# Sixteen ring places for gathered edge tiles, a fourth product bank and selector numbers from SBUF, in a four-layer graph network

## What is computed

```python
# layer 0: two relational convolutions (8 relations, 4 bases)
m   = sum(comp[etypes][:, b, None] * (h @ basis[b])[src] for b in range(4)) * norm[:, None]
h   = segment_sum(m, dst, num_segments=n) + bias + h @ loop_w
# layer 1: one relational convolution, 32 relations, 8 bases (same form, no loop)
# layer 2: mean of the neighbours and two dense products
# layer 3: four blocks of attention over the edges, each followed by a dense block
```

## Time and profile before

| | us |
|---|---|
| median of 3 runs | 3173.16 (3171.28 to 3173.49) |
| the profiled execution | 3168.56 |
| its span | 3167.1 |
| L0a, first step to last | 47.7 to 328 |
| L0b, first gather to the next load of weights | 522.0 to 798.4 |
| L1, first gather to the end of the turning | 927.9 to 1223 |
| PE busy in the span | 2981.4 (94%) |
| mean granted clock of PE | 0.985 of full speed |

### The profile page before, as it was taken

One profiled execution on the slowest core, in us unless ns is written; L12 is line 12 of the kernel. 1 busy time (PEld: TensorE's weight loads), 2 busy tenths in 40 slices (PEclk: granted clock), 3 DMA queues, 4 the chain that ended last, 5 costly groups with the idle time before them and its releaser, 6 DMA issues.

```text
span 3167.1 us, 44248 instructions
## 1 busy us (share of the span) xinstructions
PE 2981.4 (94%) x14658; PEld 2175.7 (69%) x14658; DVE 2092.7 (66%) x5078; ACT 1276.3 (40%) x2250; POOL 1166.5 (37%) x938
## 2 busy tenths in 40 slices
PE   5898998999979999999999999999999999999999
PEld 3333675444753356876458998789988899789987
DVE  7999323887348864255367678667776777767777
ACT  4666432001340033342154455345543555435554
POOL 4666236665356643441104022511135101441022
PEclk8999998999989999999999999999999999999999
DMA  2555523565236643324003001210014001130012
GB/s 81 161 163 162 174 78 122 164 170 156 79 115 169 175 129 102 96 76 145 21 30 107 12 34 50 84 53 15 31 50 129 15 8 64 43 103 15 8 64 79
DMA packets 129587, 279.39 MB, mean 88 GB/s; under 512 B 22727, under 2 KB 45575, under 8 KB 128339
## 3 DMA queue, kind: packets, MB, share of 16 engines
q0 software_dynamic: 40320, 132.15, 14.9%
q1 hardware_dynamic: 87602, 141.76, 14.4%
q10 hardware_dynamic: 1440, 2.62, 0.2%
HBM read 227.85 MB, written 27.48 MB: 81 GB/s over the span
## 4 chain that ended last, share of the span: by engine, by line
PE 77%; DVE 11%; DMA 4%; issue 3%; ACT 2%; POOL 2%; SPq 1%; DVEq 0%; another core or an unknown queue 0%; POOLq 0%; ACTq 0%
PE bank L888 16%; PE bank L155 15%; PE bank L157 15%; PE bank L156 15%; PE bank L2487 5%; PE bank L2151 2%; PE bank L1791 2%; PE bank L863 2%; DMA yT_lo<-yT_new_lo 2%; DVE G L993 1%; DVE y_tile L2103 1%; DVE y_tile L2105 1%; DVE x_stats L2086 1%; PE bank L1059 1%; DVE x_L L2318 1%
## 5 line engine op out<-in xcount | busy, mean ns | idle before, releaser
L888 PE MATMUL bank<-gathered,selector 128*128 x1328 | 655.3, 617 | 67.9 <-SPq L851 32.6
L993 DVE TENSOR_TENSOR G<-G,bank 128x512 f32 x664 | 456.1, 687 | 147.9 <-PE bank L888 114.2
L888 PEld LDWEIGHTS bank<-gathered,selector 128*128 128x128 f32 x1328 | 227.0, 193 | 340.8 <-issue 330.8
L2575 ACT CAST probT<-bank 128x512 fp32r<-128x512 f32 (+2 forms) x480 | 212.1, 516 | 263.3 <-PE bank L2487 262.4
L1459 POOL TENSOR_TENSOR weight_parts<-weight_ring,weight_parts 128x512 fp32r<-128x512 f32 x130 | 186.8, 1437 | 303.0 <-ACT weight_parts L1392 303.0
L1418 DVE TENSOR_TENSOR lhs_parts<-G,lhs_parts 128x640 fp32r<-128x640 f32 x122 | 102.3, 839 | 296.0 <-ACT lhs_parts L1390 295.8
L2657 DVE CUSTOM_DVE_ANT_0 prob<-bank,count_by_src 128x512 f32<-128x512 f32 (+1 forms) x480 | 258.3, 588 | 58.6 <-PE bank L157 58.6
L2583 DVE TENSOR_TENSOR probT<-bank,probT 128x512 fp32r<-128x512 f32 (+2 forms) x480 | 254.1, 585 | 52.5 <-ACT probT L2575 49.7
L873 ACT COPY G<-bank 128x512 f32<-128x512 f32 x160 | 82.2, 657 | 501.1 <-PE bank L863 497.4
L155 PE MATMUL bank<-weight_parts,lhs_parts 128*128 128x512 f32 x680 | 268.0, 394 | 12.6 <-POOL weight_parts L1459 7.8
L156 PE MATMUL bank<-weight_parts,lhs_parts 128*128 128x512 f32 x680 | 266.0, 391 | 0.0
(11 more groups left out here) (295 smaller groups left out, 6813.5 us busy)
## 6 DMA issues: line engine op xcount, KB each, us to landing
weight_ring<-in_L_gnn_basis SPq DMA_DIRECT2D x64, 256.0 KB, 2.7
weight_ring<-in_L_gnn_bases SPq DMA_DIRECT2D x64, 256.0 KB, 2.7
x_L<-x_rows SPq DMA_DIRECT2D x50, 256.0 KB, 4.5
x_rows<-x_L SPq DMA_DIRECT2D x50, 256.0 KB, 5.7
yT_hi<-yT_new_hi SPq DMA_DIRECT2D x4, 2560.0 KB, 11.0
yT_lo<-yT_new_lo SPq DMA_DIRECT2D x4, 2560.0 KB
count_rows<-count SPq DMA_DIRECT2D x10, 642.0 KB, 9.0
count_by_dst<-count_rows SPq DMA_DIRECT2D x10, 642.0 KB, 4.7
```

The costliest lines, as they stand in the source:

```text
L888: pe.matmul(bank[s % banks][:], sel[:, s % SELECTORS, :], xs[:, ds(slot[s % BATCH], 1), :].rearrange("p t d -> p (t d)"), start=True, stop ...
L993: dve.tensor_tensor(g, g, bank[s % banks][:], ALU.add).then_inc(*added.inc())
L2575: ins = act.copy(hi, of)
```

## The change

Three things are done in `aggregate`, all sizes otherwise the same. RING goes from 8 to 16, so the ring takes 32 KB instead of 16 KB of each partition and POOL may be 16 tiles ahead. The selectors of L0b and L1 read their numbers from the SBUF constant `C.iota`, as those of L0a do, and no longer from PSUM bank 3; DVE's copy into that bank and the wait for it go. The bank that comes free becomes the fourth for products in L0b and L1. Eight more landing events need semaphores; events of phases that follow one another now share one (`columns_converted`, `chain_made`, `small_product`), with the same waits.

```diff
-RING = 8
+RING = 16
...
-    converted, keyed, hot = C.event("edges_converted"), C.event("keys_made"), C.event("onehots_made")
-    product, taken = C.event("steps_product"), C.event("steps_taken")
+    converted, keyed, hot = C.event("columns_converted"), C.event("chain_made"), C.event("onehots_made")
+    product, taken = C.event("small_product"), C.event("steps_taken")
...
-    banks = 4 if counting else 3
+    banks = 4
     xs = M.new("gathered", [P, RING, D])
     sel = M.new("selector", [P, SELECTORS, P])
-    if counting:
-        grid = C.iota[:, 0:path.nodes]
-    else:
-        grid = bank[3][:, 0:path.nodes]
+    grid = C.iota[:, 0:path.nodes]
...
-    zeroed_act, zeroed_pool, laid = C.event("G_zero_act"), C.event("G_zero_pool"), C.event("node_grid")
+    zeroed_act, zeroed_pool = C.event("G_zero_act"), C.event("G_zero_pool")
...
     def on_dve():
         for token in ready:
             dve.wait_ge(*token)
-        if not counting:
-            dve.tensor_copy(grid, C.iota[:, 0:path.nodes]).then_inc(*laid.inc())
-            dve.wait_ge(*laid(1))
```

More of the change, by code:

```diff
@@ L1616, in __init__ @@
         self.cond_in, self.stacked = C.landed("cond_in"), C.landed("cond_stacked")
-        self.numbered, self.chain, self.angled = C.event("numbered"), C.event("cond_chain"), C.event("cond_angled")
-        self.embedded, self.projected = C.event("cond_embedded"), C.event("cond_projected")
-        self.biased, self.gated, self.halved = C.event("cond_biased"), C.event("cond_gated"), C.event("cond_hi")
+        self.numbered, self.chain, self.angled = C.event("numbered"), C.event("chain_made"), C.event("cond_angled")
+        self.embedded, self.projected = C.event("cond_embedded"), C.event("small_product")
+        self.biased, self.gated, self.halved = C.event("cond_biased"), C.event("columns_converted"), C.event("cond_hi")
         C.w2_in = C.landed("weights_in")
@@ L1754, in layer_2 @@
     bias_in = C.landed("bias_rows_in")
-    differed, degree = C.event("count_differences"), C.event("degree_chain")
+    differed, degree = C.event("count_differences"), C.event("chain_made")
     topped = C.event("count_onehots")
@@ L1758, in layer_2 @@
     x_turned, xT_act = C.event("x_turned"), C.event("xT_act")
-    by_w2, z_taken = C.event("by_w2"), C.event("taken_by_act")
+    by_w2, z_taken = C.event("small_product"), C.event("taken_by_act")
     by_w1, added = C.event("rows_multiplied"), C.event("w_added")
```

## The result

The kernel after takes 3188.87 us (median of 5 runs, 3187.16 to 3193.63) against 3173.16 us (5 runs, 3169.66 to 3175.29): 15.7 us more by the medians, ratio 1.0055 with a 95% interval of 1.0042 to 1.0067, which is 17 us. Its profiled execution has a span of 3191.5 us and is 24 us longer than that of before; it is one of the two longest of its runs, and that of before, 3168.56 us, is shorter than all five of its own, so about a third of the difference between the two profiles is scatter.

The account below looks back on a forecast made before the run. PE, busy 94%, was taken as the overall bound, with DVE slower by 0.04 us per step where PE has only steps. Banks -7.2 and ring +4.2 gave -3.0 us: 3170 us, range 3157 to 3187.

Parts of the forecast that it names:

- the price of the ring: L0b and L1: longer unbroken gathers add one late completion each, +4.2 us; bounds 0 (or a gain) and +18.8.
- late completion: L0b and L1: product issued in time but seen done some 2.1 us late; eleven and twelve places counted before the change.
- Rival 2: Longer ring fill brings two long stops per eight tiles more, 18.8 us in L0b and L1 together: 3184.8 us; chance 0.24.
- In L0a: Sixteen gathers beside the table making stay hidden in POOL's 14.43 us wait; G's clearing still starts at 46.2 us: 0.
- The fourth bank: L0b and L1: one more product in hand for PE, -4.5 and -2.7 us, together -7.2 us.
- The copy and the numbers from SBUF: L0b and L1: dropped copy hidden by the first tile's wait, 0; selectors from SBUF 0, bounds 0 and 2.5 us.
- Rival 3: DVE's selectors and POOL's gathers meet at the shared SBUF port: +12 us in all, 3185 us; chance 0.05.
- Rival 1: Ring costs nothing, 3166.0 us, or spreads gathers so late completions become fewer, 3151 us; chance 0.34, mostly near 3162.

Follow-up runs that it names:

- e1: The kernel after with the ring back at 8 places, four banks and selector numbers from SBUF kept: 3169.09 us, ratio 0.9958 to before.
- e3: The kernel after with only eight gathers ahead of L0a's tables, the other eight behind the clearing of G: 3202.76 us, ratio 1.0061 to before.
- e9: The kernel after with a ring of 8 and three banks in L0b and L1, leaving selector numbers from SBUF: 3173.65 us, ratio 1.0004 to before.
- e2: The kernel after with three product banks in L0b and L1, ring of 16 kept: 3210.00 us, ratio 1.0079 to before.
- e12: The kernel before with only a POOL clearing of 128x256 added ahead of each gather: 3148.75 us, ratio 0.9919 to before.
- e10: The kernel after with a ring of 8 and a POOL clearing of 128x256 ahead of each gather: 3139.68 us, ratio 0.9892 to before.
- e16: The kernel after with ring 8, SP's queue bringing adjacent rows instead of gathers, POOL only clearing 128x320 twice per tile: 3110.83 us, ratio 0.9804 to before.
- e8: The kernel after, ring of 16, with a POOL clearing of 128x256 ahead of every gather but the first: 3146.79 us, ratio 0.9918 to before.
- e11: The kernel after, ring of 16, with a POOL clearing of 128x320 spacing gathers at 1.52 us: 3140.99 us, ratio 0.9901 to before.
- e14: The kernel after with a ring of 8 and a POOL clearing of 128x320 ahead of each gather: 3141.57 us, ratio 0.9905 to before.

## Why the prediction was wrong

**The step that failed** is the price of the ring: "So I count one late completion more in L0b and one in L1, 2.1 us each: +4.2 us", and its bound of +18.8. Measured at four banks, 16 places against 8 cost 1.0055 - 0.9958 = 0.97%, 31 us (some 6 either way). On e1's own chip e3, which has 16 places and four banks too, took 33.7 us more than e1, and with three banks (e9 to e2) the ring costs 0.75%, 24 us. So the +4.2 was 24 to 34, and the -7.2 of the banks couldn't make up for it. I had read the rows rightly in kind: late completions follow unbroken gathers, and the largest stood behind the longest run. Then I priced a run of twice the length by the ordinary late completion of 1.9 to 2.1 us. The runs show that the wait grows with the run: in the kernel after 7.44 and 5.39 us behind 21 and 23 gathers in L0b, and 2.52, 3.98, 4.65 and 3.95 us behind 15 to 24 in L1. The stops also cost PE's clock: its mean of 0.979 in the profile of after and of 0.986 in that of e1, with levels of 1 and 0.5, means some 130 us at the lower level against 90. One stretch of it stands behind L0b's first stop, 551.4 to 568.4 us. Rival 2 was this case and gave 3184.8, against 3188.87; it had a chance of 0.24 where the rows of L1 spoke for more. That its time comes so near is in part luck: it counted 18.8 us for the ring, where 24 to 34 were measured.

**What was said against rival 2** was that L0b's first run had brought no such stop. That was no evidence: with eight places POOL first waits for a place in L0b after its twelfth gather, and that wait is what ends the run. The larger ring takes away the very wait that kept the stops short, and the first runs go to 23 and 24 gathers. For the same reason "eight tiles at 1.26 us are 10 us, about one spacing" counted a spacing that had been set by the ring.

**In L0a** I let the eight further gathers be hidden behind 14.43 us of POOL's waiting. POOL's time was free, but PE and DVE make the tables beside it, and DVE has two new waits for products there, 5.88 and 1.1 us. L0a's first step came 7.5 us later for it, of which L0a gave 3.1 back. I had named the place as a possible addition to rival 2 and counted 0.

**The fourth bank** was right in kind: -7.2 forecast, -15 (some 5 either way) measured with the ring of 8 (e9 to e1), and -8 (some 6) with the ring of 16 (e2 to after). With the gathers spread, e12 to e10, it is 0.27%, 9 us (some 7). Only the first of these says that the forecast was too small. A possible reason for more in e1 is that the forecast counted the ends of OwnProduct's stretches and three places in L1, and not that a bank more also lets PE go on during each ordinary late completion; the intervals are too wide to call that shown. It is also not seen as a smaller wait for additions: e1's groups in L0b have 8.0 us of it.

```profile
...
L885 PE MATMUL bank<-gathered,selector 128*128 x416 | 201.1, 613 | 19.1 <-DVE G L987 8.0 <-SPq L848 7.9 <-issue 2.7
...
L987 DVE TENSOR_TENSOR G<-G,bank 128x512 f32 x208 | 142.9, 687 | 58.6 <-PE bank L885 52.5 <-issue 4.5 <-remote 0.8
...
```

**The copy and the numbers from SBUF** were right: +1 us (-2 to +4) against 0, with a median of 347 ns for the selectors in all three aggregations. Selectors of up to 414 and 405 ns do appear in L0b and L1 now, where the largest was 352 ns. Rival 3, the port shared by DVE and GpSimd, is there in kind and worth next to nothing: by the mean of the groups it is 3 to 5 ns for each of 456 selectors, 2 us. It goes with the gathers: 41 of these 456 selectors take over 360 ns in the kernel after, none in e16, where POOL only clears.

**Rival 1**, in which the ring costs nothing, fell. Its mechanism, gathers that are spread and completions that come in time, is what e8 and e10 to e12 are, but a larger ring does not spread them: it lets them run on.

**Left open** is what in POOL's gathers delays PE's completions. Shown is that they come late by up to 11 us (an own product of L0b given to PE at 544.93 is signalled at 556.90 in the trace of the kernel after), that in the main this needs gathers at 1.26 us for some ten to thirty microseconds, that it mostly goes when they stand 1.46 us apart and wholly at 1.52, that half the bytes leave it as it is and that as many bytes of rows that lie together, from SP's queue, don't have it. Whether PE's work itself stands still or only its signals do is not known; DVE's signals passed in the meantime (its addition of 552.11 ends at 552.80, and PE starts behind it at 553.04). Nor is it known whether the recording of the trace has a part in it: the records of signals that are lacking are lacking where gathers run, and every run here has a recorded span and clock.

## What to carry to other kernels

A wait for a free place is also a brake. Before a ring is made deeper, ask whether it ever runs empty; if it doesn't, the only thing that more places change is how long the producer runs without a stop, and what else it disturbs then. Where one engine waits long for another that has long been given its work, look at what a third engine was doing without a break; here POOL's indirect gathers, and 0.2 us between them were worth 26 us to the kernel before. Rows that lie together can be brought by another engine's queue without the stops (e16); for scattered rows no run shows it.

## What the runs showed of the hardware that was not expected

POOL's indirect gathers of 128 rows take 0.96 us each and follow at 1.26 us. At that pitch PE's completions become late after some 10 to 20 us, by 2 us at first and by up to 11 us in runs of over 20 gathers; at 1.46 us they come in time for long (in e8 none of L0b is over 0.6 us late before 680 us, 167 us after its first gather, though one is 4.8 us late at 749), and at 1.52 us always (e11, e14). It is no matter of bandwidth: half rows (same stops) and the SP queue's full rows at 0.94 to 1.04 us (none) show that. After such stops PE's granted clock is low as well. In the window from 528 to 560 us it was 0.71 of full speed in the mean. Up to 537.7 that is the lower level, behind the wait for the first tile (the kernel before has 0.51 there, from 512 to 533); from 537.7 to 551.4 it is 1.00, and from 551.4 to 568.4, behind the first stop, 0.50. A step's product takes 2.07 us there (553.04) and 1.02 at the full clock (540.21), so a stop costs more than its wait.
